# Graph diffusion and attention on one core: the last transposes of a batch moved behind the next batch's first power product, two banks exchanged, attention events reordered

## The reference, cut to what matters

```python
# part 1, graph diffusion: eight Euler steps, linear in h
h = x @ fc_in_w.T + fc_in_b
for _ in range(8):
    f = sigmoid(alpha)[:, None] * 0.5 * (adj @ h - h) + h @ w_eff - h + x0
    h = h + f / 8
x = layernorm(x + h)
# part 2, attention with 4 heads of 32, masked by adj == 0
q, k, v = split(x @ W)
attn = softmax(q @ k.T / sqrt(32) + mask)
x = layernorm(x + attn @ v)
```

## Time and profile before

| | |
|---|---|
| median of 3 runs | 803.88 us |
| the profiled execution | 803.86 us |
| its span, first to last instruction | 802.1 us |
| TensorE matmul, busy | 88% of the span |
| TensorE weight load, busy | 65% |
| VectorE, busy | 55% |
| ScalarE, busy | 50% |
| GpSimd, busy | 9% |
| mean granted TensorE clock | 0.955 of full |

### The profile page before, as it was taken

One profiled execution on the slowest core, in us unless ns is written; L12 is line 12 of the kernel. 1 busy time (PEld: TensorE's weight loads), 2 busy tenths in 40 slices (PEclk: granted clock), 3 DMA queues, 4 the chain that ended last, 5 costly groups with the idle time before them and its releaser, 6 DMA issues.

```text
span 802.1 us, 12384 instructions
## 1 busy us (share of the span) xinstructions
PE 706.3 (88%) x3793; PEld 520.6 (65%) x3793; DVE 444.4 (55%) x1280; ACT 400.4 (50%) x903; POOL 71.1 (9%) x85
## 2 busy tenths in 40 slices
PE   5978879898998989898989989898989989899773
PEld 4756657666676757676766757576667767575542
DVE  5451226466473837465573747465664737375855
ACT  3122236546364646556463637465463646366662
POOL 4000101001010101001010101000010101000001
PEclk9999999999999999999999999999999999998988
DMA  3000030302112030403021120303021121203120
GB/s 95 1 6 9 1 81 12 88 4 73 35 47 61 24 82 0 105 0 80 24 58 46 36 69 9 95 0 92 13 72 33 49 56 32 62 0 93 34 59 27
DMA packets 37183, 35.35 MB, mean 44 GB/s; under 512 B 7584, under 2 KB 24352, under 8 KB 37152
## 3 DMA queue, kind: packets, MB, share of 16 engines
q1 hardware_dynamic: 37152, 34.96, 16.8%
HBM read 5.57 MB, written 4.19 MB: 12 GB/s over the span
## 4 chain that ended last, share of the span: by engine, by line
PE 76%; ACT 9%; issue 7%; DVE 5%; SPq 1%; DMA 1%; DVEq 0%; ACTq 0%; POOLq 0%; POOL 0%
PE psE L702 13%; PE psL L608 9%; PE psL L609 8%; PE psL L610 8%; PE psO L713 7%; ACT E L457 6%; PE psS L619 5%; PE psM L679 3%; PE psL L600 3%; PE psL L601 3%; PE psL L602 3%; PE psL L633 2%; PE psL L670 2%; PE psM L684 2%; PE psS L550 2%
## 5 line engine op out<-in xcount | busy, mean ns | idle before, releaser
L457 ACT ACTIVATE E<-Sm,negmax 128x512 f32<-128x512 f32 x256 | 183.0, 716 | 125.3 <-DVE negmax L847 113.3
L847 DVE CUSTOM_DVE_ANT_0 Sm<-psS,mask 128x512 f32<-128x512 f32 x256 | 166.8, 684 | 9.1 <-PE psS L619 6.5
L702 PE MATMUL psE<-ident,E 128*128 128x128 f32 x960 | 127.6, 276 | 4.6 <-ACT E L457 2.2
L702 PEld LDWEIGHTS psE<-ident,E 128*128 128x128 f32 x960 | 109.6, 142 | 31.3 <-issue 16.5
L880 DVE COPY ET<-psE 128x512 f32<-128x512 f32 x120 | 82.3, 686 | 83.4 <-PE psE L702 83.4
L816 DVE TENSOR_TENSOR z<-psL,z 128x512 fp32r<-128x512 f32 x48 | 33.2, 692 | 162.9 <-ACT z L450 162.9
L619 PE MATMUL psS<-Ks,Qs 96*128 96x512 f32 x256 | 99.2, 455 | 10.4 <-DVE negmax L847 6.7
L450 ACT ACTIVATE z<-psL 128x512 fp32r<-128x512 f32 x48 | 28.8, 599 | 156.5 <-PE psL L610 136.0
L394 POOL TENSOR_TENSOR rstd<-var,minus_half 128x4 f32<-128x4 f32 x32 | 32.3, 1009 | 647.0 <-DVE var L830 647.0
L505 ACT ACTIVATE ET<-psE 128x512 f32<-128x512 f32 x120 | 70.9, 591 | 12.0 <-PE psE L702 12.0
L608 PE MATMUL psL<-PTh,Yh 128*128 128x512 f32 x128 | 53.8, 420 | 18.7 <-DVE Yl L816 18.7
(11 more groups left out here) (137 smaller groups left out, 993.6 us busy)
## 6 DMA issues: line engine op xcount, KB each, us to landing
Qs<-qh SPq DMA_DIRECT2D x128, 64.0 KB, 2.0
Ks<-kh SPq DMA_DIRECT2D x128, 64.0 KB, 2.0
xin<-in_x_dram SPq DMA_DIRECT2D x16, 256.0 KB, 2.9
Qs<-ql SPq DMA_DIRECT2D x64, 64.0 KB, 2.0
Ks<-kl SPq DMA_DIRECT2D x64, 64.0 KB, 2.0
out_dram<-y SPq DMA_DIRECT2D x16, 256.0 KB, 2.3
E<-in_adj_dram SPq DMA_DIRECT2D x4, 256.0 KB, 3.6
W_sb<-in_L_gnn_W_dram SPq DMA_DIRECT2D x1, 192.0 KB, 3.3
```

Of the source, the lines that this page charges most:

```text
L457: nc.scalar.activation(E[:, h % 2, i, :], Sm[:, i % 2, :], ACT.Exp, scale=-1.0, bias=negmax[:, h * NT + i:h * NT + i + 1], accum_out=sums[ ...
L702: last = nc.tensor.transpose(e_bank(horner, i)[:, t * P:(t + 1) * P], E[:, n % 2, t, i * P:(i + 1) * P], ident[:, :])
L847: V_.tensor_tensor_reduce(out=Sm[:, i % 2, :], in0=psS[i % 2][:, :], in1=mask[:, i, :], scale=-SCALE, scalar=3e38, op0=ALU.add, op1=ALU.mi ...
```

## The change

UT leaves the tables of the polynomial's units and becomes a PREP kind, an event of the next iteration, behind the first Z1, with counters of its own (`ut_mm`, `u_ev`). It still transposes YT, which J1's evacuation fills, but into `psL[1]`. XT and Z1 exchange places and banks: Z1 is first and in bank 0, XT is HORNER 1 and in bank 1. So the numbers of the HORNER groups shift by one from there on. Who read the count of UT's evacuation from `l0_ev[0]` now reads `u_ev`. In `EVENTS` X1T comes two groups of the polynomial earlier relative to it (behind C2), Q and QL come before YT0, S 2 2 and S 2 3 stand directly before TR 2 0, K and KL before J0, LN2A behind KL, S and TR of head 3 and head 2 between J0 and C0, LN2B behind C0, V behind YT1, and J1 between the two halves of TR 3 and S0. SyncE's and GpSimd's programs are unchanged.

```diff
--- before.py
+++ after.py
@@ -43,37 +43,36 @@
 PREP, ATT, END = 1, 2, 3
 
 
-L0_UNITS = (("XT", 0), ("Z", 1), ("Z", 2), ("C", 2), ("YT", 0), ("J", 0), ("YT", 1), ("J", 1), ("UT", 0))
-L0_BANK = (0, 1, 0, 1, 1, 0, 0, 1, 0)
-L0_SPLIT = (("XT", 0), ("Z", 1), ("Z", 2), ("YT", 0), ("YT", 1))
+L0_UNITS = (("Z", 1), ("XT", 0), ("Z", 2), ("C", 2), ("YT", 0), ("J", 0), ("YT", 1), ("J", 1))
+L0_BANK = (0, 1, 0, 1, 1, 0, 0, 1)
+L0_SPLIT = (("Z", 1), ("XT", 0), ("Z", 2), ("YT", 0), ("YT", 1))
 UPB = len(L0_UNITS)
 HPB = len(L0_SPLIT)
 EPB = (L0_BANK.count(0), L0_BANK.count(1))
 
 
 EVENTS = [
-    ("HORNER", 0, 0), ("PV", 0, 0), ("PV", 1, 0), ("PV", 2, 0), ("PV", 3, 0), ("LN1A", 0, 0),
+    ("HORNER", 0, 0), ("UT", 0, 0), ("PV", 0, 0), ("PV", 1, 0), ("PV", 2, 0), ("PV", 3, 0), ("LN1A", 0, 0),
     ("HORNER", 1, 0),
     ("TR", 0, 0), ("TR", 0, 1), ("S", 1, 0), ("S", 1, 1), ("OT", 0, 0),
     ("HORNER", 2, 0),
     ("TR", 0, 2), ("TR", 0, 3), ("S", 1, 2), ("S", 1, 3), ("LN1B", 0, 0),
-    ("HORNER", 3, 0),
+    ("HORNER", 3, 0), ("X1T", 0, 0),
     ("TR", 1, 0), ("TR", 1, 1), ("S", 2, 0), ("S", 2, 1), ("CB", 0, 0),
-    ("HORNER", 4, 0), ("X1T", 0, 0),
-    ("TR", 1, 2), ("TR", 1, 3), ("S", 2, 2), ("S", 2, 3), ("LN2A", 0, 0),
-    ("HORNER", 5, 0), ("Q", 1, 0), ("QL", 1, 0),
-    ("TR", 2, 0), ("TR", 2, 1), ("S", 3, 0), ("S", 3, 1), ("LN2B", 0, 0),
-    ("HORNER", 6, 0), ("K", 2, 0), ("KL", 2, 0),
-    ("HORNER", 7, 0),
-    ("TR", 2, 2), ("TR", 2, 3), ("S", 3, 2), ("S", 3, 3), ("V", 3, 0),
-    ("HORNER", 8, 0),
+    ("HORNER", 4, 0), ("Q", 1, 0), ("QL", 1, 0), ("TR", 1, 2), ("TR", 1, 3),
+    ("HORNER", 5, 0), ("S", 2, 2), ("S", 2, 3), ("TR", 2, 0), ("TR", 2, 1), ("K", 2, 0), ("KL", 2, 0), ("LN2A", 0, 0),
+    ("HORNER", 6, 0),
+    ("S", 3, 0), ("S", 3, 1), ("TR", 2, 2), ("TR", 2, 3), ("S", 3, 2), ("S", 3, 3),
+    ("HORNER", 7, 0), ("LN2B", 0, 0),
+    ("HORNER", 8, 0), ("V", 3, 0),
     ("TR", 3, 0), ("TR", 3, 1), ("S0", 0, 0), ("S0", 0, 1),
+    ("HORNER", 9, 0),
     ("TR", 3, 2), ("TR", 3, 3), ("S0", 0, 2), ("S0", 0, 3),
-    ("HORNER", 9, 0),
 ]
 
 
 LATE_EVENTS = [
+    ("UT", 0, 0),
     ("S", 1, 0), ("S", 1, 1), ("LN1A", 0, 0), ("S", 1, 2), ("S", 1, 3),
     ("PV", 0, 0), ("PV", 1, 0), ("PV", 2, 0), ("PV", 3, 0), ("OT", 0, 0),
     ("TR", 0, 0), ("TR", 0, 1), ("TR", 0, 2), ("TR", 0, 3),
@@ -90,10 +89,10 @@
 
 
 HORNER = [
-    [("XT", 0), ("Z", 1)], [("Z", 2)], [("C", 2)], [("C", 1)], [("YT", 0)], [("XS", 0), ("J", 0)], [("C", 0)],
-    [("YT", 1)], [("J", 1)], [("UT", 0)],
+    [("Z", 1)], [("XT", 0)], [("Z", 2)], [("C", 2)], [("C", 1)], [("YT", 0)], [("XS", 0), ("J", 0)], [("C", 0)],
+    [("YT", 1)], [("J", 1)],
 ]
-PREP_KINDS = ("LN1A", "LN1B", "X1T", "Q", "QL", "K", "KL", "V", "S0")
+PREP_KINDS = ("UT", "LN1A", "LN1B", "X1T", "Q", "QL", "K", "KL", "V", "S0")
 ATT_KINDS = ("TR", "S")
 END_KINDS = ("PV", "OT", "CB", "LN2A", "LN2B")
 MPB = 4
@@ -251,6 +250,8 @@
         xin_in = [sem("xin_in0"), sem("xin_in1")]
         l0_mm = sem("l0_mm")
         l0_hi = sem("l0_hi")
+        ut_mm = sem("ut_mm")
+        u_ev = sem("u_ev")
         l0_ev = [sem("l0_ev0"), sem("l0_ev1")]
         x_high = sem("x_high")
         x_split = sem("x_split")
@@ -475,13 +476,13 @@
                     elif (kind, n) in L0_UNITS:
                         act.wait_ge(l0_mm, l0_unit(it, (kind, n)) + 1)
                         bank = L0_BANK[L0_UNITS.index((kind, n))]
-                        if kind == "UT":
-                            if not isinstance(it, int) or it > 0:
-                                act.wait_ge(x1_done, it)
-                            dst = u[:, :, :].rearrange("p t d -> p (t d)")
-                        else:
-                            dst = YT[:, :]
-                        nc.scalar.activation(dst, psL[bank][:, :], ACT.Copy).then_inc(l0_ev[bank], 1)
+                        nc.scalar.activation(YT[:, :], psL[bank][:, :], ACT.Copy).then_inc(l0_ev[bank], 1)
+                    elif kind == "UT":
+                        act.wait_ge(ut_mm, p + 1)
+                        if not isinstance(p, int) or p > 0:
+                            act.wait_ge(x1_done, p)
+                        nc.scalar.activation(u[:, :, :].rearrange("p t d -> p (t d)"), psL[1][:, :],
+                                             ACT.Copy).then_inc(u_ev, 1)
                     elif kind == "X1T":
                         act.wait_ge(m_mm, MPB * p + 1)
                         nc.scalar.activation(x1T[:, :], psM[:, :], ACT.Copy).then_inc(m_ev, 1)
@@ -628,18 +629,18 @@
                     if kind == "XT":
                         pe.wait_ge(xin_in[j], 16 * (g + 1))
                         if not isinstance(it, int) or it > 0:
-                            pe.wait_ge(l0_ev[0], l0_free(it, 0, 0))
+                            pe.wait_ge(u_ev, it)
                         for t in range(NT):
-                            last = nc.tensor.transpose(psL[0][:, t * P:(t + 1) * P], xin[:, j, t, :], ident[:, :])
+                            last = nc.tensor.transpose(psL[1][:, t * P:(t + 1) * P], xin[:, j, t, :], ident[:, :])
                         last.then_inc(l0_mm, 1)
                     elif kind == "Z":
                         if n == 1:
                             pe.wait_ge(x_split, it + 1)
                             if not isinstance(it, int) or it > 0:
-                                pe.wait_ge(l0_ev[1], l0_free(it, 1, 0))
+                                pe.wait_ge(l0_ev[0], l0_free(it, 0, 0))
                         else:
                             pe.wait_ge(l0_ev[0], l0_free(it, 0, 1))
-                        apply_power(psL[n % 2], Xh, Xl, n - 1, True).then_inc(l0_mm, 1)
+                        apply_power(psL[0], Xh, Xl, n - 1, True).then_inc(l0_mm, 1)
                     elif kind == "C" and n == 2:
                         pe.wait_ge(l0_ev[1], l0_free(it, 1, 1))
                         if isinstance(it, int) and it == 0:
@@ -659,16 +660,16 @@
                         apply_power(psL[n], Yh, Yl, PW - 1, False).then_inc(l0_mm, 1)
                     elif kind in ("YT", "UT"):
                         if kind == "UT":
-                            pe.wait_ge(l0_ev[1], l0_free(it, 1, 4))
+                            pe.wait_ge(l0_ev[1], l0_free(p + 1, 1, 0))
                         elif n == 0:
                             pe.wait_ge(l0_ev[1], l0_free(it, 1, 2))
                         else:
                             pe.wait_ge(l0_ev[0], l0_free(it, 0, 3))
-                        bank = psL[L0_BANK[L0_UNITS.index((kind, n))]]
+                        bank = psL[1] if kind == "UT" else psL[L0_BANK[L0_UNITS.index((kind, n))]]
                         for t in range(NT):
                             nodes = slice(t * P, (t + 1) * P)
                             last = nc.tensor.transpose(bank[:, nodes], YT[:, nodes], ident[:, :])
-                        last.then_inc(l0_mm, 1)
+                        last.then_inc(ut_mm if kind == "UT" else l0_mm, 1)
                     elif kind == "X1T":
                         pe.wait_ge(x1_done, p + 1)
                         for t in range(NT):
@@ -695,7 +696,10 @@
                         if not horner and not (g == NG and j == 0 and n == 0):
                             pe.wait_ge(t_ev[i % 2], evacuated - 1)
                         elif not horner and i >= 2:
-                            pe.wait_ge(l0_ev[i % 2], EPB[i % 2] * B)
+                            if i == 2:
+                                pe.wait_ge(l0_ev[0], EPB[0] * B)
+                            else:
+                                pe.wait_ge(u_ev, B)
                         elif not isinstance(evacuated, int) or evacuated > 0:
                             pe.wait_ge(t_ev[i % 2], evacuated)
                         for t in range(NT):
@@ -861,7 +865,7 @@
                         else:
                             low(psL[bank][:, :], zh[:, n, :], zl[:, n, :]).then_inc(l0_ev[bank], 1)
                     elif kind == "LN1A":
-                        dve.wait_ge(l0_ev[0], l0_free(p + 1, 0, 0))
+                        dve.wait_ge(u_ev, p + 1)
                         moments(0, p, lambda t: u[:, t, :])
                     elif kind == "LN1B":
                         dve.wait_ge(x1_kept, p)
```

## The result

The changed kernel takes 885.24 us (median of 4 runs, 880.81 to 885.88) against 804.38 us before: ratio 1.099, 95% interval 1.0947 to 1.1034. That is +80.9 us where +65.8 was forecast; the time lies in the stated range of 838 to 890 us, near its upper end. The profiled execution took 885.88 us, its span is 884.1.

The account below looks back on a forecast made before the run. TensorE's work (88% busy) and its stand-stills were taken as the bound. Twelve batches at +5.2 us (62.4), plus 9.2 for the last, less 5.8, made +65.8: 803.9 to 869.7 us, range 838 to 890.

Parts of the forecast that it names:

- Part 1: Batch boundary: with UT behind the next Z1 and banks exchanged, stand-still and half clock go, gaining 4.03 us each.
- the first rival: Whole kernel: new waits are hidden and each boundary gives 4.03 us back, 750 us; chance 0.04.
- X1T: Behind C2, X1T waits for LN1B on VectorE: 1.0 us, bounds 0 to 1.5.
- The TR wait: Before TR of head 2, TensorE stands still 3.3 us for the last exponential, behind three VectorE steps.
- The S0 wait: Before the first S0: late LN2B delays SyncE's store and the stacking behind it; 4.25 us, bounds 2.5 to 5.5.
- The half clock: TensorE at lower clock after the new waits: 1.41 us behind TR of head 2, 1.1 behind the first S0.
- The sum: Batch grows from 44.45 to 49.65 us, +5.2; with the loop's ends +65.8 us in all, giving 869.7.
- the second: Before S0: stacking lands in time, only the TR and X1T waits stand, 800 us; chance 0.08.
- the third: No half clock behind the new waits, batch 47.15 us, 837 us; chance 0.13.
- The fourth: Clock stays low longer, 1.4 us a batch, 888 us; chance 0.12.

Follow-up runs that it names:

- part 1 alone: Kernel before the change with only UT behind the next Z1, XT behind PV and banks exchanged, attention events unmoved: 749.5 us, ratio 0.931.
- the queue's order: Changed kernel with SyncE issuing the stacking transfers of Qs and Ks before the store of y in iterations with a polynomial: 811.56 us, ratio 1.0072.
- an early y: Changed kernel with LN2A moved behind CB and LN2B behind KL on VectorE, SyncE's store still ahead of the stacking: 814.38 us, ratio 1.0121.
- kernel with both waits filled: Changed kernel plus discarded matmuls, eight before TR 2 0 and twelve before the first S0 of the thirteen full batches: 840.47 us, ratio 1.0438.
- kernel with both waits away: Changed kernel with TR 2 0 and TR 2 1 behind J0, and the stacking issued before the store: 768.28 us, ratio 0.9541.

## Why the prediction was right, and where it was off

*Part 1*: right. The stand-still and the half clock behind it were priced at 2.62 + 1.41 = 4.03 us; part 1 alone shortened the batch by 4.1 and the kernel to 749.5 us, where the first rival, which is this part without new waits, had stood at 750.

*X1T*: right, 1.0 us forecast, 0.97 measured.

*The TR wait*: right, 3.3 forecast, 3.29 measured. Three VectorE steps and the 1.17 us from a maximum to the TR are all in it.

*The S0 wait*: the mechanism was right and is shown twice, by the queue's order and by an early y. From the end of TR 3 1 (396.56 + 0.79) to S0 it is 4.04 us, of which the row counts 3.79 as idle; forecast was 4.25. The kernel with both waits filled shows the distances without half clock: from TR of head 2 to TR of head 3 it is 425.56 - 414.45 = 11.1 us where 38.7 - 26.8 - 1.41 = 10.5 were laid out, and to S0 15.9 where it was 15.5. So TensorE came 0.6 us later to the wait and y 0.4 later, small misses that nearly cancel in the wait and add 0.4 us to the batch.

*The half clock*: the term that was mis-sized. I priced it at 1.41 + 1.1 = 2.5 us a batch from one stand-still of before. The filled waits put it at 44.8 us; over the fourteen TR waits and thirteen S0 waits that is 20 / 14 = 1.4 and 25 / 13 = 1.9 us, 3.3 a batch. I had argued that part of the low stretch would fall into the longer wait and be harmless. Instead the low stretch can be twice as long, 6.8 us and not the 3.4 of the boundary wait that I had priced it from: 18.28 - 15.88 = 2.4 us were lost behind one TR, next to nothing behind another. Part of the 25 us behind S0 is that same effect; what chooses between the lengths, or no low stretch, isn't shown.

*The sum*: a batch was to be 49.65 us. Ten batches of the change, from 179.51 to 687.33, are 50.78 us each. The 1.13 us more, in twelve batches, are 13.6 us, and the thirteenth adds another 1.1: together nearly all of the 15.1 us between forecast and result. The first rival fell because the events do wait, the second because the stacking does stand behind the store; the third because the half clock is there, 44.8 us of it. The fourth, a longer low stretch at 888 us, came nearest to the measured 885 and had been given 0.12. The forecast's own range, 855 to 883, misses the measurement; the stated one holds it because it took in most of that rival.

The Trainium skill's remark in "DMA: Bandwidth & Descriptors", section "Issuing engines are not separate DMA queues", that the time to initiate a DMA is usually small beside the DMA itself, doesn't fit this queue's trace: one issue takes 0.59 us against 2.0 to landing, and from the store's issue to that of head 0's sixth transfer it is 399.25 - 395.52 = 3.7 us. Those 3.7 us are most of the 6.03 us from LN2B's end to S0.

## What to carry to other kernels

An order that is walked by several engines must be followed on each of them, and on the queues that it doesn't list: here the costliest effect sat in a program that the change didn't touch, behind a store whose landing nothing needs soon. Before a piece is moved away, ask which wait it covers; V, Q and J0 were each the cover of something. And don't price a stand-still of TensorE by its length alone: the granted clock fell behind all thirteen S0 waits of 3.5 to 5.2 us in the change but behind only ten of its fourteen TR waits of 3.1 to 3.3 us, behind eight of twelve waits of 1.75 us and four of the 1.30 us ones, and the loss was up to seven tenths of the wait again. Last, look at what runs on the other engines at a piece's new place: y took twice its time wherever it met Xl.

## What the runs showed of the hardware

The half clock can be bought off. With 112 matmuls more, whose results are thrown away, the changed kernel was 20 us faster, and with 268 more it was 44.8 us faster, at a mean granted clock of 0.985 against 0.923. The waits of 1.38 and 0.97 us that were left beside them brought no half clock, and neither did J0's 1.03 us in part 1 alone; but 1.30 us brought it in four batches of the kernel with both waits away, so no length of wait that was seen here separates the two cases cleanly. Behind stand-stills of 3.3 us the loss varied from nothing to 2.4 us between batches that are alike otherwise, and so two batches of the changed kernel in a row took 51.35 us (383.30 to 434.65) and 49.07 us (434.65 to 483.72).

VectorE's four instructions for y take 1.11 us by themselves and 2.0 to 2.1 us in all 36 batches, of three kernels, in which they overlap GpSimd's Xl.
